# The seam between two program blocks: a late root moved ahead of scatters and of a chain of links, more idle matmuls on TensorE, and a load in eight parts

## The reference, cut to what matters

```python
x = x + gnn0(layernorm(x), adj)            # adj @ (x @ W) + b
x = x + ffn0(layernorm(x), ...)            # attention, then 8 experts, top 2
x = x + gnn1(layernorm(x), adj)            # adj scaled by 1/sqrt of the row sums
x = x + ffn1(layernorm(x), ...)            # router, 6 experts, top 2

# ffn0's experts
probs = softmax(flat @ router_w.T); tp, ti = top_k(probs, 2)
tp = tp / (sum(tp) + 1e-9)
out = sum over e of weights[:, e] * ((silu(flat @ w1[e].T) * (flat @ w3[e].T)) @ w2[e].T)

# gnn1
d_inv_sqrt = (sum(adj, axis=-1) + 1e-5) ** (-0.5)
```

## Time and profile before

| What | Value |
|---|---|
| Time, median of 3 runs | 855.65 us (854.5 to 856.88) |
| Profiled execution, its own time | 856.57 us |
| Its span, from first to last instruction | 854.5 us |
| PE busy | 811.8 us, 95% of the span |
| DVE busy | 697.2 us, 82% |
| ACT busy | 517.9 us, 61% |
| POOL busy | 426.2 us, 50% |
| Mean granted TensorE clock | 0.992 of full speed |

### The profile page before, as it was taken

The page is one execution under the profiler, slowest core; times in us unless marked ns, Lnnn a source line. Parts: engine busy times, 40 slices in busy tenths (PEclk is TensorE's granted clock), DMA queues, the critical chain, the costliest instruction groups (busy, mean ns, idle before and its releaser), DMA issues.

```text
span 854.5 us, 21578 instructions
## 1 busy us (share of the span) xinstructions
PE 811.8 (95%) x6292; PEld 628.6 (74%) x6293; DVE 697.2 (82%) x2699; ACT 517.9 (61%) x1072; POOL 426.2 (50%) x410
## 2 busy tenths in 40 slices
PE   6988999999888899999999999899999999999998
PEld 6666777767547899999999999566666666666663
DVE  4899898989767698877777888888888888888863
ACT  3667778787546466556565654556555556655654
POOL 4248888888777200930100052566665566666300
PEclk9999999999999999999999999999999999999999
DMA  9603311131115766676666662333333344443322
GB/s 270 177 18 90 99 51 53 46 115 42 44 41 171 196 190 172 173 195 167 173 169 167 173 181 73 112 122 125 122 124 119 118 144 152 140 131 121 108 88 99
DMA packets 104711, 108.25 MB, mean 127 GB/s; under 512 B 27278, under 2 KB 88672, under 8 KB 102464
## 3 DMA queue, kind: packets, MB, share of 16 engines
q1 hardware_dynamic: 94096, 88.52, 35.8%
q0 software_dynamic: 8880, 18.19, 7.1%
q10 hardware_dynamic: 1664, 0.66, 0.3%
HBM read 82.07 MB, written 25.26 MB: 126 GB/s over the span
## 4 chain that ended last, share of the span: by engine, by line
PE 62%; issue 3%; POOL 1%; DVE 1%; DMA 1%; SPq 0%; ACT 0%; POOLq 0%; DVEq 0%; ACTq 0%
PE banks L2062 17%; PE banks L2102 10%; PE banks L2228 9%; PE banks L2220 9%; PE banks L2196 7%; PE banks L2077 2%; PE banks L2123 2%; PE banks L2134 1%; PE banks L2151 1%; PE banks L2242 1%; PE banks L2163 1%; POOL expert_rows L1345 1%; PE banks L2172 1%; PE banks L2143 1%; DMA slots_out<-ys 0%
## 5 line engine op out<-in xcount | busy, mean ns | idle before, releaser
L1345 POOL DMA_INDIRECT expert_rows<-slots_out,slot_c x128 | 141.8, 1108 | 75.9 <-DVE ys L1601 43.9
L326 POOL DMA_INDIRECT slots_in<-flat,slot_now x115 | 120.7, 1050 | 35.7 <-issue 31.2
L2062 PE MATMUL banks<-xT_hi,w_hi 128*128 128x256 f32 (+1 forms) x426 | 126.8, 298 | 0.4 <-DVE w_lo L1620 0.4
L2062 PE MATMUL banks<-xT_hi,w_lo 128*128 128x256 f32 (+1 forms) x426 | 120.5, 283 | 0.0
L2062 PE MATMUL banks<-xT_lo,w_hi 128*128 128x256 f32 (+1 forms) x426 | 120.2, 282 | 0.0
L2102 PE MATMUL banks<-w_sb,prod 128*128 (+1 forms) x852 | 107.7, 276 | 2.7 <-DVE ys L1601 2.7
L2102 PEld LDWEIGHTS banks<-w_sb,prod 128*128 128x128 f32 (+1 forms) x852 | 101.8, 192 | 3.3 <-issue 3.1
L2062 PEld LDWEIGHTS banks<-xT_hi,w_hi 128*128 128x128 f32 (+1 forms) x426 | 76.0, 178 | 0.6 <-issue 0.6
L2062 PEld LDWEIGHTS banks<-xT_lo,w_hi 128*128 128x128 f32 (+1 forms) x426 | 76.4, 179 | 0.0
L2062 PEld LDWEIGHTS banks<-xT_hi,w_lo 128*128 128x128 f32 (+1 forms) x426 | 76.1, 179 | 0.0
L1419 ACT ACTIVATE w_hi<-w_raw 128x684 fp32r<-128x684 f32 x71 | 54.9, 773 | 26.6 <-PE banks L2062 26.2
(11 more groups left out here) (305 smaller groups left out, 2117.7 us busy)
## 6 DMA issues: line engine op xcount, KB each, us to landing
f_all<-gates_dram SPq DMA_DIRECT2D x16, 1536.0 KB, 6.1
w_raw<-in_w SPq DMA_DIRECT2D x71, 342.0 KB, 3.4
xs<-slots_in SPq DMA_DIRECT2D x71, 128.0 KB, 2.6
slots_out<-ys SPq DMA_DIRECT2D x71, 128.0 KB, 3.2
base_all<-in_x SPq DMA_DIRECT2D x16, 256.0 KB, 4.1
out<-ob SPq DMA_DIRECT2D x16, 256.0 KB
slots_in<-zrow SPq DMA_DIRECT2D x20, 128.0 KB
adjt<-in_adj_t SPq DMA_DIRECT2D x32, 64.0 KB, 2.4
```

The costliest lines, as they stand in the source:

```text
L326: G.indirect_dma_start(out=slots_in, out_offset=bass.IndirectOffsetOnAxis(ap=slot_now0[g % 2][:, n:n + 1], axis=0), in_=flat[g % 2][:, n / ...
L1345: G.indirect_dma_start(out=rows[p][:, n, :], out_offset=None, in_=slots_out[0:filled(g) * R, :], in_offset=bass.IndirectOffsetOnAxis(ap=sl ...
L2062: last = T.matmul(banks[bank][0:m, half * R:(half + 1) * R], ww[:, par, n * HIDP + c * P:n * HIDP + c * P + m], xx[:, par, :], start=q == ...
```

## The change

Four edits, all at or before the seam, and one that adds matmuls behind it.

- `REST14` takes the scatters 3 and 6 of group 14 too: only its scatter 0 stays ahead of the root of group 15, and POOL issues seven of group 14's scatters behind the boundary instead of five.
- `scale_top(NG - 4, NG)` moves from the end of DVE's chain of links to its head. The shift of `cnti` and the copy to `nblk` move behind the boundary, to the head of `table_of_blocks(0)`; `cnti` therefore becomes a tensor of the whole program, and the count `TABLE` of the links grows by two. The copy of `table`'s first eight entries moves to the start of the first block.
- `opening(6, ...)` becomes `opening(10, ...)`, `fill_up(5)` becomes `fill_up(8)`, and `fill_up(3)` comes between the first block's transposes and the second's.
- `adjn` is loaded in eight parts of 256 KB after the adjacency of groups 6 to 13.

```diff
-        REST14 = (4, 2, 5, 1, 7)
+        REST14 = (3, 6, 4, 2, 5, 1, 7)
+        cnti = sb("cnti", [P, 8], i32)
...
                     for g in range(5, NG):
                         load_adj(g)
-                        if g == 8:
-                            sp.dma_start(adjn[:, :, :], adj_t.rearrange("(t p) n -> p t n", p=P)).then_inc(ld_adjn, 16)
+                        if 6 <= g < 14:
+                            part = slice((g - 6) * 8, (g - 5) * 8)
+                            sp.dma_start(adjn[:, part, :], adj_t.rearrange("(t p) n -> p t n", p=P)[:, part, :]).then_inc(ld_adjn, 16)
...
                         V.tensor_copy(maskb[:, :], cst[:, C_MASK:C_MASK + NN]).then_inc(dve_w, 1)
+                        V.tensor_copy(table[:, 0, 0:8], cst[0:1, C_IOTA:C_IOTA + 8])
...
+                    scale_top(NG - 4, NG)
                     dve.wait_ge(pe_t, 3)
                     link(V.tensor_scalar(full[:, :], banks[B_COUNT][0:1, 8:16], float(R), -16.0 * 2 * TG, ALU.is_ge, ALU.mult))
                     link(V.tensor_scalar(due[:, :], full[:, :], 16.0 * TG * NG, None, ALU.add))
                     link(V.scalar_tensor_tensor(fill[:, :], banks[B_COUNT][0:1, 0:8], float(R), cst[0:1, C_BASE:C_BASE + 8], ALU.max, ALU.add))
                     link(V.tensor_scalar(cnti[:, :], banks[B_COUNT][:, 0:8], 1.0, float(R - 1), ALU.max, ALU.add))
-                    link(V.tensor_scalar(cnti[:, :], cnti[:, :], 8, None, ALU.arith_shift_right))
-                    link(V.tensor_copy(nblk[:, :], cnti[:, :]))
-                    link(V.tensor_copy(table[:, 0, 0:8], cst[0:1, C_IOTA:C_IOTA + 8]))
-                    scale_top(NG - 4, NG)
...
-                            pe.wait_ge(ld_adjn, 16)
+                            pe.wait_ge(ld_adjn, 16 * 8)
...
-                    opening(6, B_PRT[0])
+                    opening(10, B_PRT[0])
...
-            tabled, TABLE = sem("tabled"), 20
+            tabled, TABLE = sem("tabled"), 22
...
                         if step == 0:
+                            link(V.tensor_scalar(cnti[:, :], cnti[:, :], 8, None, ALU.arith_shift_right))
+                            link(V.tensor_copy(nblk[:, :], cnti[:, :]))
...
                         block_of(k, u)
-                    fill_up(5)
+                        if isinstance(k, int) and k == 0:
+                            fill_up(3)
+                    fill_up(8)
                     blocks(pe, block_and_first, 2)
```

More of the change, by code:

```diff
@@ L178, in build @@
             sel_all = sb("sel_all", [P, NG + 1, TG + 1, 8], bf16)
-            full, cnti = sb("full", [1, 8]), sb("cnti", [P, 8], i32)
+            full = sb("full", [1, 8])
             LN = ((0,), (1,), (2, 3), (4, 5, 6), (7, 8, 9), (10, 11, 12), (13, 14, 15))
```

## The result

The changed kernel took **864.39 us** (median of 9 runs, 862.35 to 867.31), the kernel before, beside it on the same chip, 856.94 (9 runs). The ratio is 1.0082, with a 95% interval of 1.0061 to 1.0103: slower by 7 us. Forecast were 854.9 us, 852.8 to 856.5, and "no change". The profiled executions span 865.3 and 854.5 us; that of the changed kernel, at 867.31 us, is the slowest of its nine, so the traces differ by more than the medians do.

What follows compares the result with a forecast made beforehand. Bound: SP's release at block 8, at 281.9 us. It comes 0.8 us earlier, the start costs 0.1, so 0.7 us less than the median of 855.65: 854.9 us, range 852.8 to 856.5.

Steps and rivals of the forecast that it cites:

- the one on the boundary: End of the first block: TensorE drains last, and the boundary moves from 257.89 to 257.15, 0.73 us earlier.
- The idle of 1.79 us: GpSimd's idle ahead of a scatter: if it came before the root instead, the root would still start by 254.1.
- The rival with a late boundary: Boundary does not move, so the last scatters hold SP 0.8 us longer than before: 856.5 us, chance 0.15.
- The root and its price: GpSimd's last root before the boundary starts with its input, taking 1.07 us; at 2.11, the boundary comes 0.3 later.
- The openings, `scale_top`, the links: Before the boundary: twenty openings take 2.5 us, `scale_top` runs first, DVE's links end at 256.85, PE restarts at 257.46.
- The clock: TensorE behind the boundary: with gaps filled no half-clock stretch; with the first transposes, 1.2 us earlier by block 4.
- The second stretch: TensorE's half-clock stretch from 288.80 to 292.10, behind the wait for the store: expected to stay, as nothing fills that gap.
- the rival of the clock in full: The second half-clock stretch goes too, saving 1.65 us: 853.3, or 852.8 with the zero rows' 0.4; chance 0.15.
- The scatters as SP's releaser: At block 8 the last scatter, landing after 3.0 us, releases SP at 281.1 instead of 281.9: 0.8 us earlier.
- the zero rows': ACT's last zero rows, issued at 277.5 instead of 278.69, land after 3.19 us at 280.7, before the last scatter.
- The start and `adjn`: The `table` copy at the first block's start costs 0.1 us; loading `adjn` in eight parts neither costs nor gains.

Runs made afterwards that it cites:

- the run with the gather: The changed kernel plus one gather of 128 rows into a spare tile, ahead of the last scatter before the boundary: 856.25 us, ratio 1.0001.
- without the drain: The changed kernel with its first block closed without GpSimd's drain: 860.01 us, ratio 1.0047.
- with the root ahead of two scatters: The changed kernel with scatters 3 and 6 of group 14 behind the last root but ahead of the boundary: 860.87 us, ratio 1.0047.
- with 115 ahead and memsets: The changed kernel with five scatters behind the boundary as before, and four memsets between the last scatter and the root: 858.16 us, ratio 1.0011.

## Why the prediction was wrong, step by step

**The step that failed** is the one on the boundary: "PE thus becomes the last engine at the boundary, ahead of DVE's 256.85." It was worked out from the ends of VectorE's, ScalarE's and TensorE's work, and GpSimd was taken as done with its root. Its drain has no row in the timeline, and in the trace before it ended 0.34 us after the root, hidden under the other engines. What it costs depends on what GpSimd has issued: 0.34 us there, 9.31 us here. The hint was in the rows: "The idle of 1.79 us has no releaser in the profile". I asked only whether it would come in front of the root. It is the price at which the 114th scatter pays off the 113 ahead of it, and the change moved this scatter behind the boundary, so that the drain paid instead, five times as much. The rival with a late boundary ("say because DVE or POOL drains late") named the right engine and priced it at 0.7 us; it needed one of 7.6.

**The root and its price** were right: it started with its input and took 1.04 us (1.07 taken). What made the row of 2.11 us can be read from the traces. Of their 320 roots 45 took longer than 1.1 us, and just these began while VectorE ran `qk_rot`, a sum of two tiles of 128x1024; the less of it was left, the shorter the root. From the kernel before, and from the run with eight scatters behind:

```profile
234.44 1.23 DVE L581 TENSOR_TENSOR qk_rot<-qk_cos,qk_sin 128x1024 f32<-128x1024 f32 x1
```

```profile
234.01 1.23 DVE L584 TENSOR_TENSOR qk_rot<-qk_cos,qk_sin 128x1024 f32<-128x1024 f32 x1
234.55 1.60 POOL L318 TENSOR_TENSOR rr<-ssv,mhalf 128x4 f32<-128x4 f32 x1
```

The Trainium skill ("SBUF — State Buffer", "SBUF: two separate sides") has a VectorE instruction with two inputs in SBUF hold the port pair that it shares with GpSimd for its whole length; these rows agree with it. Beside the moved root VectorE ran no `qk_rot`, and `ohr`, its two-input instruction of 0.22 us there, began 0.69 us into the root, which still took 1.04; nor does a hold of `ohr` by the root show, which by the same rule the root, having begun first, would cause (0.22 us, 0.23 before with no root beside it). So 2.11 was not a price that this root could meet at its place.

**The openings, `scale_top`, the links** were right. Twenty openings took 2.48 us (2.5 forecast). With the debt paid off, in the run with the gather, TensorE restarts at 258.10 with the root's input 0.69 us later than before (254.53 against 253.84): 257.41 on the old scale, where 257.46 had been worked out.

**The clock.** "With the gaps filled I expect no such stretch": right where the boundary did not wait long for GpSimd (1.00 from 262 to 275 us with five and with six scatters behind, without the drain, and with the gather ahead of the last scatter); with the root ahead of two scatters and with 115 ahead and memsets that window shows 0.87. The second stretch stayed in the run with the gather (0.90 from 275 to 292 us), as forecast. With five behind it went as well, and 0.23% of 855.65 are 2.0 us: this comes near the rival of the clock in full (2.35 us), but with the scatters left where they were. In the changed kernel the clock fell twice, for 6.8 us each, the first time over the wait for the drain.

**The scatters as SP's releaser** were right, in the changed kernel and in the run with the gather. There the last one lands at 282.35, 281.66 on the old scale, against 281.1: the landing took 4.21 us, where I had taken 3.0 and bounded it by 3.9. This term was mis-sized, and so was the zero rows': issued at 277.94, 277.25 on the old scale (277.5 forecast), the last of them took 4.1 us to land, not 3.19. So nothing is left of the 0.7 us of gain, and the ratio of 1.0001 is what "same" meant.

**The start and `adjn`.** The root's input came at 253.25 in the run without the drain and at 257.82 in the one with nothing but REST14 changed, with others between; a tenth of a microsecond at the start can't be told from that. No wait in the changed kernel names `adjn`.

## What to carry to other kernels

An engine's end at a block boundary is its drain, not its last row: look up the drain's own record, engine by engine, and how far behind the last row it ends, before moving work off the one that seems to wait. On GpSimd, count the transfers of one kind that stand ahead of the drain, and read an idle time marked "issue" ahead of a transfer as a cost that will turn up elsewhere when the transfer is moved. Where such a debt stands at a boundary, one small transfer of another kind ahead of the last ones paid it off here for 1.06 us and half a microsecond of stall; of all versions the ones with five and with six scatters behind, all else as in the change, were the fastest, 0.2% under the kernel before and no more.

## What had not been expected of the hardware

GpSimd's drain took 0.082 us per scatter issued since the last clearing, though these had landed long before: 9.31 us with 113, while no DMA queue of the core moved anything. A drain cleared the count, and so did a gather into another tile (the 12 ahead of it, without a visible wait; 112 for half a microsecond: 0.78 us of idle behind the gather instead of 0.30), and the 114th scatter in a row, for 1.8 us between scatters and 2.42 behind the root. The 114th of 128 gathers waited likewise, 1.50 us, in every trace. Not shown is what makes a transfer one "of another kind": the gathers and the two scatters put in differed from the program's own in the DRAM tensor, the index tile and partly in direction, all at once. Another semaphore or another buffer of a tile is not enough, since the program's scatters and gathers alternate between two of each and were counted on. Nor is it shown what the 113 stands for; it was met at two places, both with transfers of 128 rows. And why the run without the drain lost 0.5% is explained by its trace in part: the first scatter came 3.43 us behind TensorE's restart, and the rest was not taken apart.
